# The causal mask of five of eight attention heads, made by GpSimd on the exponentials in place of a mask product on TensorE

## The reference

```python
s = jnp.einsum('bhid,bhjd->bhij', q * mult, k * mult)
mask = (jnp.arange(t)[:, None] < jnp.arange(t)[None, :]).astype(s.dtype)
s = s - jnp.asarray(INFTY_APPROX, s.dtype) * mask[None, None]
p = jax.nn.softmax(s, axis=-1)
o = jnp.einsum('bhij,bhjd->bhid', p, v)
```

## Time and profile before

| | |
|---|---|
| three runs | 1150.01, 1147.92, 1147.56 us; median 1147.92 us |
| the profiled execution | 1151.88 us, of which the span of the profile 1150.1 us |
| PE busy over the span | 1033.8 us (90%) |
| ACT | 967.2 us (84%) |
| DVE | 921.6 us (80%) |
| POOL | 827.4 us (72%) |
| PE's granted clock | 1.00 from 0 to 830 us, 0.87 from there on |

### The profile page before, as it was taken

One profiled execution on the slowest core, in us unless ns is written; L12 is line 12 of the kernel. 1 busy time (PEld: TensorE's weight loads), 2 busy tenths in 40 slices (PEclk: granted clock), 3 DMA queues, 4 the chain that ended last, 5 costly groups with the idle time before them and its releaser, 6 DMA issues. The chain is left out here.

```text
span 1150.1 us, 27366 instructions
## 1 busy us (share of the span) xinstructions
PE 1033.8 (90%) x7462; PEld 796.3 (69%) x7462; DVE 921.6 (80%) x2636; ACT 967.2 (84%) x3519; POOL 827.4 (72%) x1198
## 2 busy tenths in 40 slices
PE   5899999999999999999999999999889897988600
PEld 2478888788888788888788888888645443577500
DVE  5888998999998999888888888887658756667555
ACT  6899999999999999999999999997779786887433
POOL 4665578888888888788887788887366775666634
PEclk9899999999999999999999999999989998999955
DMA  5410000100000100000000000000433322310166
GB/s 147 126 43 13 13 18 25 34 25 25 24 22 25 34 15 15 15 13 16 18 13 15 16 13 17 17 15 16 124 99 97 116 84 71 92 54 29 31 223 216
DMA packets 54056, 58.17 MB, mean 51 GB/s; under 512 B 8060, under 2 KB 42991, under 8 KB 53908
## 3 DMA queue, kind: packets, MB, share of 16 engines
q1 hardware_dynamic: 36756, 35.37, 10.3%
q0 software_dynamic: 8704, 16.87, 4.5%
q10 hardware_dynamic: 8448, 4.20, 1.2%
HBM read 33.21 MB, written 24.23 MB: 50 GB/s over the span
## 5 line engine op out<-in xcount | busy, mean ns | idle before, releaser
L737 ACT ACTIVATE squares<-unit 128x128 f32<-128x128 f32 x1024 | 272.9, 301 | 7.0 <-PE unit L1192 7.0
L559 POOL TENSOR_TENSOR roped<-roped,rope_b 128x512 f32<-128x512 f32 x128 | 170.0, 1328 | 90.2 <-DVE rope_b L1083 87.1
L737 ACT ACTIVATION_READ_ACCUMULATOR squares<-unit 128x1 f32 x1024 | 233.6, 234 | 0.0
L1536 POOL DMA_INDIRECT y_rows<-y_out,place_y x144 | 156.4, 1086 | 90.6 <-issue 44.9
L1066 DVE TENSOR_TENSOR roped<-unit,cos_sb 128x512 f32<-128x512 f32 x256 | 174.2, 681 | 31.5 <-ACT squares L737 30.3
L1083 DVE TENSOR_TENSOR rope_b<-unit,sin_sb 128x512 f32<-128x512 f32 x256 | 173.9, 679 | 0.0
L715 ACT ACTIVATE probs<-scores,rr 128x256 f32<-128x256 f32 x256 | 123.7, 483 | 51.9 <-issue 26.3
L1272 PEld LDWEIGHTS unit<-ident,roped 128*128 128x128 f32 x1024 | 118.0, 142 | 31.0 <-ACT k_t L754 12.3
L1035 DVE SCALAR_TENSOR_TENSOR acc<-pv,den,acc 128x128 f32<-128x128 f32 x448 | 138.7, 340 | 0.4
L1272 PE MATMUL unit<-ident,roped 128*128 128x128 f32 x1024 | 135.4, 276 | 0.6 <-POOL roped L559 0.5
L567 POOL TENSOR_TENSOR roped<-roped,rr 128x1024 f32<-128x1024 f32 x64 | 121.6, 1900 | 9.6 <-DVE roped L1092 8.9
(11 more groups left out here) (301 smaller groups left out, 2987.9 us busy)
## 6 DMA issues: line engine op xcount, KB each, us to landing
shared<-y_rows SPq DMA_DIRECT2D x16, 512.0 KB, 5.5
x_all<-in_L_attn_x SPq DMA_DIRECT2D x32, 128.0 KB, 2.2
h_late<-in_L_ffn_W SPq DMA_DIRECT2D x16, 256.0 KB
out_x<-sums ACTq DMA_DIRECT2D x16, 256.0 KB, 3.6
rope_b<-x_rows SPq DMA_DIRECT2D x13, 258.0 KB
tile_x<-x_rows SPq DMA_DIRECT2D x12, 258.0 KB
y_rows<-y_out,place_y POOLq DMA_INDIRECT x144
x_rows<-filler SPq DMA_DIRECT2D x16, 129.0 KB
```

The costliest lines, as they stand in the source:

```text
L559: pool.tensor_tensor(out=roped[parity][:, u, heads], in0=roped[parity][:, u, heads], in1=rope_b[:, u % 2, heads], op=ALU.add).then_inc(S[" ...
L737: nc.scalar.activation(squares[:, c * D:(c + 1) * D], UN[0][:, c * D:(c + 1) * D], ACT.Square, accum_out=ssq[parity][:, u * H + c:u * H + ...
L1536: pool.indirect_dma_start(out=y_rows, out_offset=bass.IndirectOffsetOnAxis(ap=place_y[i % (2 * SLOTS)][:, s:s + 1], axis=0), in_=y_out[at] ...
```

## The change

For heads 0, 1, 2, 5 and 6 (`ZEROED`) the mask product is left out, so that the exponentials are taken of unmasked scores, and POOL then sets the entries above the diagonal of both diagonal blocks of `probs` to zero, with one `affine_select` on 128 x 2 x 128 fp32 elements in place, at a place in its order that is fixed by hand. PE's product of values times exponentials waits for that instruction (`masked`) in place of the exponentials (`exp_done`). Heads 3, 4 and 7 stay as they were.

```diff
+        ZEROED = (0, 1, 2, 5, 6)
@@ POOL
+                def zero_future(h):
+
+                    if C:
+                        wait(pool, "exp_done", 2 * (H * (n - 2) + h + 1))
+                        diagonal = probs[:, h % NPR, :].rearrange("p (a c) -> p a c", c=P)[:, 0:3:2, :]
+                        pool.affine_select(out=diagonal, in_=diagonal, compare_op=ALU.is_ge, fill=0.0, base=0,
+                                           pattern=[[0, TT], [1, P]], channel_multiplier=-1).then_inc(S["masked"], 1)
...
+                zero_future(0)
                 if rest:
                     scatter(n - 7, other, 1, 0)
                 if X or A or B or C or R or N2:
                     roots()
+                zero_future(1)
                 if R:
                     gated_residual()
                 if X or A or B or C or R or N2:
                     newton()
                     offsets()
+                zero_future(2)
                 if rest:
                     scatter(n - 7, other, 1, 1)
...
+                zero_future(5)
                 if A:
                     add(4)
                 if now:
                     scatter(n - 6, parity, 0, 1)
+                zero_future(6)
@@ PE, values_times_probs
-                    wait(pe, "exp_done", 2 * (g + 1))
+                    if h in ZEROED:
+                        wait(pe, "masked", len(ZEROED) * b + ZEROED.index(h) + 1)
+                    else:
+                        wait(pe, "exp_done", 2 * (g + 1))
@@ PE, scores
-                        nc.tensor.matmul(diagonal, ident_bf[:, :], mask, start=True, stop=False)
-                        nc.tensor.matmul(s[:, 0:P], k[:, h, 0:P], q[:, h, 0:P], start=False, stop=False)
-                        nc.tensor.matmul(s[:, T:T + P], k[:, h, P:T], q[:, h, P:T], start=False, stop=True)\
+                        alone_s = h in ZEROED
+                        if not alone_s:
+                            nc.tensor.matmul(diagonal, ident_bf[:, :], mask, start=True, stop=False)
+                        nc.tensor.matmul(s[:, 0:P], k[:, h, 0:P], q[:, h, 0:P], start=alone_s, stop=alone_s)
+                        nc.tensor.matmul(s[:, T:T + P], k[:, h, P:T], q[:, h, P:T], start=alone_s, stop=True)\
                             .then_inc(S["s_done"], 1)
```

More of the change, by code:

```diff
@@ L260, in adaln_block @@
             out_stored2 out_stored3 late_var late_guess late_root late_xn late_turned late_h2 late_logits late_max
-            late_less late_exp late_back late_rows late_score late_gap late_tanh late_best late_which late_chosen
+            late_less late_exp late_back late_rows late_score late_gap late_tanh late_best late_which late_chosen masked
             late_counts br_parted late_prefix late_place late_tagged late_weights late_scattered""".split()
```

## The result

The changed kernel takes 1163.75 us, the median of 4 runs (1158.23 to 1168.38), against 1148.97 us for 4 runs of the kernel before (1147.56 to 1154.54): a ratio of 1.0109, 95% interval 1.0071 to 1.0147. The prediction had the direction (slower, 0.49) and the ring that sets the new period, but not who waits in it, and was too small: 1152.7 us, range 1136 to 1160, and the measured time lies outside that range.

What follows compares the result with a forecast made beforehand. PE bounds the kernel at 24.56 us a step, and a POOL and DVE ring takes over. Weight-piece steps + 4.8, late steps + 1.8, early steps - 1.8 sum to + 4.8 on 1147.9: 1152.7 us, range 1136 to 1160.

Steps and rivals of the forecast that it cites:

- the ring: POOL and DVE's loop from one step's last key sum to the next; claimed 24.7 us late, 25.0 with a weight piece.
- the two estimates beside it: Cost of one 256-column select by the skill's cycles per element: 0.40 us unrolled, 0.50 us not.
- The round from the key sum to the scaling: POOL's stretch from last key sum to first scaling: 7.56 - 0.45 + 1.17 = 8.28 us, missing slot 0's query sum.
- A piece step: A step with a weight piece: 10.8 + 14.21 = 25.0 us, + 0.44 in each of 11 steps, + 4.8.
- So now DVE is first.: Slot 2 of a late step: DVE's query sum at 8.13 precedes POOL's scaling at 8.28, which waits; period 24.7 us.
- DVE's 8.13: DVE's arrival at slot 2's query sum after the last key sum: 8.07 plus 0.06 to PE's turning of keys.
- rival (b): In between: scaling still precedes DVE's query sum, slot 1 costs nothing; late step 24.41 us, total 1145.9 us; 25%.
- The round by that section in the prediction: With SBUF ports locked until 115 ns after DVE's query sum ends, the scaling starts later: a round 0.26 us longer.
- PE's new waits for `masked` cost nothing as such.: PE's values-times-exponentials products: selects finish before use, select 0 near 517.5 against 519; cost 0.
- the four early steps: Steps before the scatters, period 23.16 us: PE gets its 0.44 us relief in each, - 1.8 in all.
- Selects 5 and 6 are free.: Selects around the key sums, where POOL waits for DVE: no cost, against + 1.17 us for selects 0, 1 and 2.
- (d): More collisions, such as slot 3's query sum with the second scaling: each 0.5 us a round; 1157 to 1166 us; 12%.

Runs made afterwards that it cites:

- e4: Changed kernel with all eight mask products kept on PE and the five selects run as well; 1134.26 us, ratio 1.015 to the kernel before.
- e2: Changed kernel with GpSimd masking heads 0, 1 and 2 only, without the selects for 5 and 6; 1129.27 us, ratio 1.0104 to the kernel before.
- e1: Changed kernel with GpSimd masking heads 5 and 6 only, without selects 0, 1 and 2; 1115.29 us, ratio 0.9982 to the kernel before.
- e5: Changed kernel with POOL's first scaling of a step made to wait for DVE's query sum of slot 2; 1178.27 us, ratio 1.0231 to the kernel before.
- e11: e9 with the last two sequences masked on PE as before; 1158.43 us, ratio 1.0013 to the kernel before.
- e9: Changed kernel with POOL's gated residual moved from ahead of the Newton step to behind the second scaling; 1161.8 us, ratio 1.0037 to the kernel before.
- e3: Changed kernel with neither select nor mask product for the five heads; 1108.65 us, ratio 0.9917 to the kernel before.
- e7: e6 with each scaling also split into two instructions of four heads; 1172.76 us, ratio 1.0174 to the kernel before.
- e6: Changed kernel with `place_k` put ahead of the first scaling on POOL; 1160.48 us, ratio 1.0098 to the kernel before.
- e12: e11 with GpSimd masking heads 0 and 2 alone; 1149.99 us, ratio 0.9934 to the kernel before.
- e8: Control: the kernel before with `place_k` first and each scaling in two halves; 1150.12 us, ratio 1.0001 to the kernel before.

## Why the prediction was right, and where it failed

**Right.** That a ring of POOL and DVE takes the period over from PE (e4: PE's relief is worth 0.02). Which selects count most (e2 has 0.30 of the 0.39, e1 no loss). A select is 0.41 us where I took 0.43 from the earlier trace rows; of the two estimates beside it, 0.40 and 0.50, the first fits. The round from the key sum to the scaling, 8.43 for 8.28: the query sum of slot 0 wasn't missed but cost L512 0.27 (0.52 for 0.25), and the selects were a little cheaper.

**Right by luck.** A piece step is 25.07 where I had 25.0: + 5.7 in 11 steps (from - 1.03 to + 4.68) for my + 4.8. POOL is first there too, by 0.02 us, so the figure is near by another road.

**Failed: "So now DVE is first."** This is the step that made the late steps too short, 24.7 for 24.95. DVE's 8.13 was 8.07 plus "0.06 from the key sum to PE's turning". The 8.07 is exact (631.11 - 623.04), but PE turns the keys of slot 1 0.43 after the key sum, since ACT's copy of slot 0, at which PE stood already in the kernel before, comes last there. DVE is there at 8.50, POOL at 8.43. POOL wins by 0.07 us and DVE pays the whole scaling. With POOL first the prediction's own terms give 8.28 + 2.74 + 13.90 = 24.92, close to the 24.95 measured; rival (b) had this order, but took no collision ahead of it (7.77 to the scaling) and so came to 24.41. And if DVE had been first, 24.7 would still have been wrong: e5 shows that the sum for "DVE first" was 0.7 short, 0.37 of it that same turning, 0.24 the release of SBUF, which I took at 0.55 after the query sum's start from the earlier trace rows and which a waiting scaling in e5 got 0.10 after its end. The Trainium skill ("SBUF — State Buffer", section "SBUF: two separate sides") gives about 0.115 us after the end for the loser of the ports; e5's wait is for a semaphore as well, so that it agrees but doesn't prove the rule, and the 0.24 may be the price of that wait. The round by that section in the prediction, 24.7 + 0.26, lies near 24.95 too, but for an order that didn't occur: that is luck. The 12 steps from 445.92 to 740.29 and the two behind them brought + 6.1 (4.68 to 10.79) for my + 1.8, of which 5.0 in the 12 and 1.1 in the two, where the kernel before had steps below its period (23.98 and 24.34).

**Failed: "PE's new waits for `masked` cost nothing as such."** True in the middle of the stage, false in its last sequence, which I didn't look at. From 10.79 at the last `half_vx` but one the lag grows to 14.81 at the end, + 4.0 us for my 0. Most of it are PE's waits of 0.93 and 1.81 us for selects queued behind a scatter and the roots, the residual and the Newton step of POOL. e11 ends attention 4.6 us earlier than e9.

**Mis-sized: the four early steps.** Each was to give 0.44 us, the whole relief of PE. The earlier trace rows give 23.16 for one; in the changed kernel the rows of POOL's L512 are

```profile
78.19 0.25 POOL L512 TENSOR_TENSOR vx<-ssq,rms_eps 128x32 f32<-128x32 f32 x1
...
101.20 0.25 POOL L512 TENSOR_TENSOR vx<-ssq,rms_eps 128x32 f32<-128x32 f32 x1
```

23.01 apart. It comes to - 1.03 in all for my - 1.8. The selects are not what is missing: e3, with none, has 23.02 there too, and in a late step 24.2 to 24.3 where PE's own 24.12 was my term. What holds the early steps at 23.0 was not looked for.

**Failed: "Selects 5 and 6 are free."** They stand outside POOL's part of the ring, but make `one_hot` longer, which lies in DVE's part. In the changed kernel that is the 0.09 us a step between it and e2. In e9 and e11, where `one_hot` takes 1.13, it keeps most of the gain away. In e1 it is the smaller part: masks 5 and 6 are worth little there, since slot 7 waits for DVE without any select too (e3).

The terms measured: - 1.0 early, + 5.7 with pieces, + 6.1 late, + 4.0 at the end, + 14.8 in the profiled executions, for my - 1.8 + 4.8 + 1.8 = + 4.8. The medians differ by 14.8 as well; that the two agree so closely is chance, as the part behind attention varies by more. Of the rivals (d), more collisions, has the measured time in its 1157 to 1166, of which my range took only the lower third, not most. Its example, slot 3, is not what happened: that query sum lasts 0.70.

## What to carry to other kernels

Price an instruction that is added to an engine with idle time by the loop that it lies in: follow each engine from one wait to the next round to the same point, and put beside it every pair of instructions that want SBUF at the same time, since their order can turn on 0.07 us and cost a whole instruction. Follow each arrival time back to the engine that comes last, not to the nearest one. And look at the last round by itself: what is hidden in the steady state is bare there.

## What the runs showed of the hardware

- Back-to-back instructions of POOL keep SBUF together against a waiting DVE: the query sum took 2.75 us before two halves of 2.04 us together (e7), 2.60 behind a `place_k` of 0.26 and a scaling of 1.90 (e6). Yet in the changed kernel DVE got in between the scaling and `place_k`, which then took 0.72. What tells the cases apart was not settled.
- A DVE instruction of 32 columns with two SBUF inputs can cost over twice its time: `one_hot` 0.55 us in e12, 1.13 in e9.
- A select of 128 columns takes 0.288 us, one of 256 takes 0.41.
- The part behind attention, from the start of DVE's last sum into `acc` to the end of the span, takes 298.0 to 298.9 us in e1 to e4, but 324.7 to 334.9 in e5 to e8 and 333.5 to 343.3 in e9 to e12. So it differs between chips, and on two of them by 10 us between executions that do the same work there. The mean granted clock from the last `half_vx` on is 0.89 in e4, 0.90 in the changed kernel and 0.88 in e5. POOL's scatters of results wait 5.5 us for `y_out` in e4 and 43.3 in e5. The cause is open.
